# Softmax maximum carried as rows of the query stack in two of three attentions, one broadcast copy on VectorE, output bias on GpSimd, later weights in six portions

## What is computed

```
x = x + _L0_xattn_ref(_layernorm(x, axis=-1), ctx_1024, ctx_1024, ...)   # 16 heads of 8
x = x + _L0_ffn_ref(...)                                                 # 8 experts, top 2
x = x + _L1_xattn_ref(_layernorm(x, axis=-1), ctx_1024, ...)             # the same, with rotary positions
x = x + _L1_ffn_ref(...)                                                 # quantised
x = x + _L2_xattn_ref(_layernorm(x, axis=-1), ctx_1024, ctx_1024, ...)   # one key/value head for 16 query heads, biases
x = x + _L2_ffn_ref(...)
x = x + _L3_xattn_ref(...)                                               # one head of 128
x = x + _L3_ffn_ref(...)
# a 16-head attention:
scores = einsum('bhqd,bhkd->bhqk', q, k) / sqrt(8)
out = einsum('bhqk,bhkd->bhqd', softmax(scores), v) @ Wo.T (+ bo in layer 2)
```

## Time and profile before

| what | value |
|---|---|
| median of three runs | 1574.77 us (1566.39 to 1575.15) |
| the profiled execution | 1575.81 us, its span 1574.0 us |
| PE, DVE, ACT, POOL busy over the span | 81%, 60%, 44%, 32% |
| row maxima on DVE (L501) | x384, 687 ns each |
| second matmuls with `pick_head` on PE (L629) | x1536, 512 of them in each of A0, A1, A2 |
| A0: first score matmul to last `scoresT` | 44.0 to 244.8 us |
| A1: the same | 600.1 to 826.5 us |
| A2: the same | 913.6 to 1112.3 us |

### The profile page before, as it was taken

The page is one execution under the profiler, slowest core; times in us unless marked ns, Lnnn a source line. Parts: engine busy times, 40 slices in busy tenths (PEclk is TensorE's granted clock), DMA queues, the critical chain, the costliest instruction groups (busy, mean ns, idle before and its releaser), DMA issues. The chain is left out here.

```text
span 1574.0 us, 38722 instructions
## 1 busy us (share of the span) xinstructions
PE 1268.9 (81%) x12718; PEld 1023.4 (65%) x12718; DVE 947.0 (60%) x2946; ACT 688.8 (44%) x1442; POOL 496.8 (32%) x564
## 2 busy tenths in 40 slices
PE   3899995439979958889996689999799865489991
PEld 1677883328869926677783367778577665478981
DVE  2567765624544347778855567777477767676452
ACT  1456662125535503345563346666333353144440
POOL 2222201541445255422301132220111112776065
PEclk9999996559999967789998879999799987599996
DMA  5775633011223236436420044332200031134342
GB/s 141 172 217 149 172 99 121 27 54 49 80 75 103 80 104 155 108 94 164 109 79 1 14 113 126 81 101 70 81 0 0 22 113 67 61 111 123 106 140 77
DMA packets 120187, 147.93 MB, mean 94 GB/s; under 512 B 14560, under 2 KB 100726, under 8 KB 113956
## 3 DMA queue, kind: packets, MB, share of 16 engines
q1 hardware_dynamic: 111876, 129.97, 29.4%
q0 software_dynamic: 8192, 16.46, 3.8%
HBM read 95.79 MB, written 50.92 MB: 93 GB/s over the span
## 5 line engine op out<-in xcount | busy, mean ns | idle before, releaser
L501 DVE TENSOR_REDUCE A_neg_max<-A_s_bank 128x4 f32<-128x512 f32 x384 | 260.1, 687 | 139.3 <-PE A_s_bank L614 135.2
L376 ACT ACTIVATE A_probsT<-A_st_bank 128x512 f32<-128x512 f32 x384 | 227.6, 598 | 84.8 <-PE A_st_bank L629 78.1
L627 PE MATMUL A_st_bank<-A_q_stack,A_k_stack 72*128 72x128 bf16 x1536 | 226.1, 225 | 2.0 <-ACT A_max_partsT L370 1.1
L629 PE MATMUL A_st_bank<-A_max_partsT,pick_head 96*128 96x128 bf16 x1536 | 225.6, 224 | 0.0
L614 PE MATMUL A_s_bank<-A_k_stack,A_q_stack 72*128 72x128 bf16 x1536 | 158.2, 229 | 22.3 <-DVE A_neg_max L501 18.0
L627 PEld LDWEIGHTS A_st_bank<-A_q_stack,A_k_stack 72*128 72x128 bf16 x1536 | 157.2, 104 | 28.1 <-issue 26.3
L629 PEld LDWEIGHTS A_st_bank<-A_max_partsT,pick_head 96*128 96x128 bf16 x1536 | 154.4, 101 | 9.6 <-issue 8.0
L614 PEld LDWEIGHTS A_s_bank<-A_k_stack,A_q_stack 72*128 72x128 bf16 x1536 | 112.1, 102 | 34.1 <-DVE A_neg_max L501 23.8
L640 PE MATMUL A_pv_bank<-A_probsT,A_v_pad 128*32 128x128 f32 x3072 | 128.9, 285 | 0.0
L1933 ACT ACTIVATE E_h<-E_h_bank,w_L_b 128x256 f32<-128x256 f32 x184 | 76.9, 472 | 85.7 <-PE E_h_bank L2036 84.8
L2036 PE MATMUL E_h_bank<-E_xT,E_w_u 128*128 128x256 f32 x368 | 92.1, 396 | 7.9 <-issue 7.2
(11 more groups left out here) (363 smaller groups left out, 2775.8 us busy)
## 6 DMA issues: line engine op xcount, KB each, us to landing
A_q_stack<-q_scratch SPq DMA_DIRECT2D x48, 576.0 KB
A_k_stack<-k_scratch SPq DMA_DIRECT2D x32, 576.0 KB
q_scratch<-A_q_parts SPq DMA_DIRECT2D x48, 192.0 KB, 2.3
A_ctxT<-in_ctxT SPq DMA_DIRECT2D x33, 256.0 KB, 6.8
E_xe<-slots_in SPq DMA_DIRECT2D x53, 128.0 KB, 2.1
slots_out<-E_ye SPq DMA_DIRECT2D x53, 128.0 KB, 1.7
k_scratch<-A_k_parts SPq DMA_DIRECT2D x32, 192.0 KB
q_scratch<-A_q_parts SPq DMA_DIRECT2D x48, 128.0 KB, 2.2
```

What stands on the lines that cost most here:

```text
L376: act.activation(probsT[n % 2][:, c * HQ:(c + 1) * HQ, :], st_bank[c % 2][:, :].rearrange("k (a q) -> k a q", a=HQ), ACT.Exp, scale=scale) ...
L501: dve.tensor_reduce(neg_max[:, c * HQ:(c + 1) * HQ], s_bank[c % 2][:, :].rearrange("q (a k) -> q a k", a=HQ), AX.X, ALU.max, negate=True). ...
L627: pe.matmul(dst, k_stack[slot][:, h % kheads, at:at + S], q_stack[slot][:, h, at:at + S], start=True, stop=False)
L629: last = pe.matmul(dst, core.pick_head[:, h, :], max_partsT[n % 2][:, :], start=False, stop=True)
```

## The change

In A0 and A2 (`spread = not rope`) the second matmul goes away. The stacks have 128 rows: 72 of data, 24 plus 32 more in the query stack and 56 in the key stack. Rows 96 to 127 of the query stack hold the maxima (high parts of the 16 heads, then low parts), the same rows for every head; rows 72 to 127 of the key stack hold a constant of zeros and ones (`pick_rows`) that picks a head's two rows. The constants are made once at the start, stored to DRAM (`pick_dram`) and loaded by SP into the four slots (`constants`). Per batch one DVE copy (`spread_max`) repeats the 32 rows of `max_rows` for 16 heads; it stands behind `divide` and `place(0)`. `scores` still uses 72 rows. For the constants to fit, A2's key stack gets a copy of the key rows for every head, in three DMAs per half. A2's output bias is added to x by POOL, four batches at a time, not by DVE batch by batch. `load_rest` is cut into six portions, one ahead of each of the groups 2 to 7, largest weights first. A1 keeps its second matmul.

```diff
-        k_stack = [sb(f"k_stack{i}", [COMBO, kheads, HALF], BF16) for i in range(4)]
+        k_stack = [sb(f"k_stack{i}", [S if spread else COMBO, NH, HALF], BF16) for i in range(4)]
...
+                    if shared:
+                        rows = dram[p][half].rearrange("i d t -> (i d) t")
+                        span = rows.shape[1]
+                        each = bass.AP(tensor=rows.tensor, offset=rows.offset, ap=[[span, 3 * DH], [0, NH], [1, span]])
+                        for i in range(3):
+                            sp.dma_start(dest[i:COMBO:3, :, :], each).then_inc(stack_loaded[slot], 16)
...
+            def constants(slot):
+
+                if spread:
+                    flat = lambda t: t.rearrange("r h t -> r (h t)")
+                    sp.dma_start(flat(k_stack[slot][COMBO:S, :, :]), core.pick_dram).then_inc(stack_loaded[slot], 16)
+                    sp.dma_start(flat(q_stack[slot][COMBO:hi, :, :]), core.pick_dram[0:hi - COMBO, :])\
+                        .then_inc(stack_loaded[slot], 16)
...
             load_ctx(0, 0, 0)
             prep(0)
+            constants(2)
+            constants(3)
             prep(1)
-            if load_rest:
-                load_rest(sp)
             for g in range(2, NG):
+                if load_rest:
+                    load_rest(sp, g - 2, NG - 2)
                 prep(g)
...
+            def add_bias(g):
+
+                if shared_kv:
+                    pool.wait_ge(xn_done, g + 1)
+                    core.settle(pool)
+                    x4 = core.x_group(g).rearrange("t (b d) -> t b d", b=GB)
+                    pool.tensor_tensor(x4, x4, shared_kv[3][:, None, :].to_broadcast([S, GB, D]), ALU.add)\
+                        .then_inc(bias_added, 1)
...
+            def spread_max(b, n):
+
+                dve.wait_ge(mt_copied, b + 1)
+                dve.tensor_copy(q_stack[n // 2 % 4][MAX_ROWS, 0:BY_DVE, n % 2 * S:(n % 2 + 1) * S],
+                                max_rows[n % 2][MAX_ROWS, None, :].to_broadcast([2 * NH, BY_DVE, S])).then_inc(m_spread, 1)
...
                     divide(b)
-                    add_bias(b)
                     place(0)
+                    if spread and has_scores(b + 1):
+                        spread_max(b + 1, n + 1)
...
                 if c == 0:
-                    pe.wait_ge(mt_copied, b + 1)
+                    pe.wait_ge(m_spread if spread else mt_copied, b + 1)
...
-                    pe.matmul(dst, k_stack[slot][:, h % kheads, at:at + S], q_stack[slot][:, h, at:at + S],
-                              start=True, stop=False)
-                    last = pe.matmul(dst, core.pick_head[:, h, :], max_partsT[n % 2][:, :], start=False, stop=True)
+                    last = pe.matmul(dst, k_stack[slot][:, h, at:at + S], q_stack[slot][:, h, at:at + S],
+                                     start=True, stop=spread)
+                    if not spread:
+                        last = pe.matmul(dst, core.pick_head[:, h, :], max_rows[n % 2][:, :], start=False, stop=True)
...
+                sp.wait_ge(picked, 1)
+                sp.dma_start(core.pick_dram, wide_pick[:, :, :].rearrange("r h t -> r (h t)")).then_inc(pick_stored, 16)
                 sp.wait_ge(x_loaded, 16)
+                sp.wait_ge(pick_stored, 16)
...
+                dve.tensor_copy(wide_pick[:, :, :], narrow_pick[:, :, None].to_broadcast([S - COMBO, NH, HALF]))\
+                    .then_inc(picked, 1)
```

More of the change, by code:

```diff
@@ L90, in multi_head_attention @@
     kd = DH if shared_kv else D
-    kheads = 1 if shared_kv else NH
+    vheads = 1 if shared_kv else NH
+    spread = not rope
+    MAX_ROWS = slice(S - 2 * NH, S) if spread else slice(0, 96)
+    BY_DVE = NH
     if rope:
@@ L144, in multi_head_attention @@
         neg_max = sb("neg_max", [S, NH], F32)
-        max_parts = sb("max_parts", [S, 96], BF16)
-        max_partsT = [sb(f"max_partsT{i}", [96, S], BF16) for i in range(2)]
+        max_parts = sb("max_parts", [S, MAX_ROWS.stop], BF16)
+        max_rows = [sb(f"max_rows{i}", [MAX_ROWS.stop, S], BF16) for i in range(2)]
+        hi, lo = MAX_ROWS.start, MAX_ROWS.start + (NH if spread else 32)
         outT = sb("outT", [128, HQ, S], F32)
@@ L347, in _ @@
                     split_rest(pool, own, q_f, q_parts, D, g + 2, QL, q_lead, q_split)
+            for g in range(2):
+                add_bias(g)
             first = own.n
@@ L369, in copy_max @@
                 act.wait_ge(mt_ready, b + 1)
-                act.copy(max_partsT[q][:, :], wo_bank16[0:96, 0:S]).then_inc(mt_copied, 1)
+                if spread and not (isinstance(b, int) and b < 2):
+                    act.wait_ge(m_spread, b - 1)
+                act.copy(max_rows[q][MAX_ROWS, :], wo_bank16[MAX_ROWS, 0:S]).then_inc(mt_copied, 1)
             def exps(b, n, c):
@@ L522, in divide, with add_x @@
                                   sums[:, :, :, None].to_broadcast([S, 4, HQ, DH]), ALU.mult).then_inc(o_norm, 1)
-            def add_bias(b):
-                if shared_kv:
-                    own.did(dve.tensor_tensor(core.x_tile(b - 1), core.x_tile(b - 1), shared_kv[3], ALU.add))
-            def add_x(b):
-                if shared_kv:
-                    own.wait()
+            def add_x(b, n=0):
+                if shared_kv and n % GB == 1:
+                    dve.wait_ge(bias_added, add_x.it * 2 + n // GB + 1)
                 dve.wait_ge(wo_ready, START + b + 1)
@@ L640, in probs_v @@
                     last = pe.matmul(pv_bank[a * VW:(a + 1) * VW, c * S:(c + 1) * S],
[L641 removed]
+                                     v_pad[p][:, n % GB, h % vheads, :], probsT[n % 2][:, h, :], start=True, stop=True)
                 if c == 3:
@@ L2747, in program, with load_rest @@
         first_loads = [load for load in loads if load[2] in needed_first]
-        rest_loads = [load for load in loads if load[2] not in needed_first]
-        def load_rest(sp):
-            for dst, src, _ in rest_loads:
+        size = lambda load: math.prod(n for _, n in load[0].ap)
+        rest_loads = sorted((load for load in loads if load[2] not in needed_first), key=size, reverse=True)
+        def load_rest(sp, part=0, parts=1):
+            for dst, src, _ in rest_loads[part::parts]:
                 sp.dma_start(dst, src).then_inc(rest_loaded, 16)
@@ L2760, in load_expert @@
             sp.dma_start(exp_w1[:, at], ap["L0_exp_w1"].rearrange("d e f -> d (e f)")[:, at]).then_inc(exp_w1_loaded, 16)
-        with nc.sbuf_tensor("wide_pick", [96, NH, S], F32) as wide_pick, nc.Block() as block:
-            first_loads.append((wide_pick[:, :, :], ap["pick_head"], "wide_pick"))
+        picked = ctx.enter_context(nc.semaphore("picked"))
+        pick_stored = ctx.enter_context(nc.semaphore("pick_stored"))
+        with nc.sbuf_tensor("narrow_pick", [S - COMBO, NH], F32) as narrow_pick,\
+                nc.sbuf_tensor("wide_pick_head", [96, NH, S], F32) as wide_pick_head,\
+                nc.sbuf_tensor("wide_pick", [S - COMBO, NH, HALF], BF16) as wide_pick, nc.Block() as block:
+            first_loads.append((narrow_pick[:, :], ap["pick_rows"], "narrow_pick"))
+            first_loads.append((wide_pick_head[:, :, :], ap["pick_head"], "wide_pick_head"))
             @block.sync
@@ L2842, in shape_constants @@
     c = {"ident": np.eye(128, dtype=np.float32)}
+    pick = np.zeros((56, 16), np.float32)
+    for part in range(2):
+        pick[24 + 16 * part:40 + 16 * part, :] = np.eye(16, dtype=np.float32)
+    c["pick_rows"] = pick
     pick = np.zeros((96, 16, 128), np.float32)
```

58 lines of the change are left out of this document (35 added, 23 removed).

## The result

The changed kernel takes 1563.65 us (median of 14 runs, 1559.65 to 1567.09) where the kernel before, on the same chip, takes 1574.47 (14 runs): a ratio of 0.9936, 95% interval 0.9925 to 0.9947. It is faster, by 10 to 11 us and not by the 41 of the forecast. That is inside the wide range of 1514 to 1566 us, at its slow end, which was there for a rival, and outside the forecast's own 1523 to 1548. The profiled execution took 1563.3 us, with a span of 1561.4.

What follows compares the result with a forecast made beforehand. PE's instruction stream was taken to bound A0 and A2. Gains of 20 and 5.5 us in A0 and 25 in A2, less 9.5 of costs, made 41: from 1575.8 to 1535 us, own range 1523 to 1548, wide range 1514 to 1566.

Steps and rivals of the forecast that it cites:

- PE's work: A0 and A2 loops: sixteen fewer matmuls save PE 0.94 us per batch, 3.76 per group, leaving 20.8 in A0.
- The copy's length: The new DVE copy of 2048 columns, each batch in A0 and A2: taken as 0.70 us.
- The rivals with 1.22 and 2.2 us: Slower DVE copy: at 1.22 us the kernel takes 1566 us, chance 0.14; at 2.2 us 1631, chance 0.07.
- The copy itself waits for ACT's copy of the maxima: DVE copy in the loop: ACT's copy ends at 105.38, the division at 105.36, so waiting costs nothing.
- Waits of 1.2 us per group: A0 loop: PE and DVE do not hide each other fully; 1.2 us of waits make the group 22.0 us.
- The loss mostly passes on: A2: the 0.19 us per batch lost behind POOL moves to `normalise` in the second batch, which meets the same instruction.
- DVE per plain batch: Batch without preparation: DVE carries 3.5 us, with the copy and its semaphore 4.3, against PE's 4.43.
- Bias: A2: moving the output bias from DVE to POOL gains DVE 0.2 to 0.3 us per batch; group 22.1 us.
- Portions: A0: later weights in portions let the context load go out near 64 us, recovering the whole 5.5 us lost.
- Starts: Start costs: opening 3 us, first `scoresT` 1.5 in each of two attentions, A2's key loads 3.5; 9.5 in all.
- the stacks have slack too: Weights in portions, A0: the stack loads can bear the new order of DMAs, so the 5.5 us is taken whole.
- the second one: POOL or DMA takes part back: 0.3 us per copy behind POOL, 19 us, 1554; or late A2 stacks, 1553; chance 0.16.

Runs made afterwards that it cites:

- half_copy: The changed kernel with the DVE copy writing 8 of 16 heads, constants for the rest: 0.9922 of the kernel before, 12.0 us less.
- pool_waits: The changed kernel with POOL's key split waiting until the group's normalised x is written: 0.9924 of the kernel before, 15.4 us less.

## Why the prediction was wrong, and where it was right

- **PE's work** (right, in part by luck): 20.8 us a group forecast, 21.1 measured (95.07 of 108 us, times 23.93). The matmuls of 128 rows cost nothing extra: they come 0.056 us from start to start, those before 0.058. But the 20.8 were the old period less 3.76 and held 0.7 us of PE's waits (it was busy 105.04 of 108 us, 23.9 per group), so by busy time 20.1 were due. The other 1.0 us fits the way of counting, since before each wait the last matmul counts to its end, 0.22 us, and not to the next start; that is an estimate.
- **The copy's length** (right): 0.70 us forecast, 0.69 measured where nothing is in its way, 0.42 for 1024 columns. The rivals with 1.22 and 2.2 us fall.
- **"The copy itself waits for ACT's copy of the maxima, which ends at 105.38 where the division ends at 105.36, so this costs nothing"** (wrong, the step that failed first, and the largest cause that was shown). It is true of the batch whose rows were read. In the third batch ACT's two query copies stand ahead of that copy, and it costs 1.62 us, with 0.37 more because the copy then meets POOL; taking it out gave 0.89 us of period in A0 and 10 us in all. Before the change nothing on DVE hung on this ACT copy, so the trace of before could show no wait; the order of ACT, with place(0) ahead of `copy_max`, could.
- **Waits of 1.2 us per group** (wrong): 2.9 in A0, 3.1 in A2. Of the 1.93 us over the forecast of A0, the ACT order is 0.89, POOL in the way of `normalise` 0.64, and 0.40 stay in the run with both repaired; of the 2.51 of A2 they are 0.56, 0.60 and 1.34. Over 8 groups of each, the loops missed the forecast by 35.5 us: 21.6 of them are these two causes, and the cause of the other 14 stays open. The time is only some 30 us off because the portions gave 4 us more than forecast.
- **"The loss mostly passes on"** (right in kind, not carried into the sum): POOL's key split lengthens `normalise` from 1.11 to 1.75 us. It was named, and the sum has no term of its own for it in A0.
- **DVE per plain batch** (a little low): 4.3 forecast, 4.55 measured back to back, above PE's 4.43. The two engines were taken as 19.5 and 20.8 us; by the measured rows DVE's is 18.2 + 1.5 + 1.1 = 20.8 without any delay, so the slack of 1.3 us was not there. This alone doesn't explain the miss: half_copy took 1.1 us of work off DVE and gave 0.28 in A0, all in the batch without preparation. In the others it is the waits of one engine for another that count.
- **Bias** (a little high): 0.2 to 0.3 us per batch taken, 0.67 per group (0.17 per batch) measured with the copy.
- **Portions** (right, 5.5 us in the kernel before): 5.5. In the changed kernel without them the context load comes later still, so that they keep off 9 to 10. From 84 to 90 us, where the granted clock was 0.54, it is 1.00 in the changed kernel, as forecast.
- **Starts** (the sum right, its terms less so): 9.5 forecast, 9.4 measured. The opening was taken at 3 us and cost 1.9 (SP's first A0 load at 18.53, not 16.62), of which 1.5 are left at the first scores; the first `scoresT` of A2 cost 2.9 where 1.5 was taken. Group 1's stacks went out 8 us later, which was not foreseen ("the stacks have slack too").
- **Rivals**: the 19 us of the second one come nearest in kind (POOL takes a part back), yet the larger part of what was shown was ACT's order, which no rival named. DMA did not take part in the steady loop: PE had no stack wait from 92 to 200 us at a DMA share of 0.68, nor from 950 to 1080 at 0.61. Ahead of it PE did wait for stacks, 1.58 us at 69.7 in A0, 2.6 and 1.6 at 905 and 931 in A2, which the prediction had named as a sign of being wrong.

The sum by measured terms: 8 x 0.60 + 8 x 0.66 + 5.5 - 9.4 = 6.2, against 10 to 11. With the portions at the 9.9 us that they are worth here by the ratios (0.9999 - 0.9936, of 1574.47) it is 10.6.

## What to carry to other kernels

When an engine takes over a step, its new instruction inherits a producer: follow that producer's order through every phase of the loop (here four batches), not the one batch with the cleanest rows. Where two engines come within some per cent of each other, add up both with start-to-start times over a whole period before calling one the bound, since a delay may then reach the time; and take a little work off each in turn to see in which batches it does. And cost the starts as carefully as the loop: here they ate what 512 x 2 removed matmuls gave.

## What the runs showed of the hardware that was not expected

- A VectorE copy whose source repeats (32 x 128 read 16 times, bfloat16 to bfloat16) runs as fast as a plain one would: 0.69 us for 2048 columns and 0.42 for 1024, 0.26 ns per column, half of the 0.514 of the cast from float32. The Trainium skill ("VectorE: DVE Perf Modes", the perf-mode tier table) gives 693 ns for such a copy without repetition, and the trace agrees.
- The same copy took up to 1.08 us, and `normalise` (four instructions) 1.75 and not 1.11, where a POOL instruction of 1.16 us ran. The Trainium skill ("SBUF — State Buffer", on the shared port pair) has them exclude each other for a whole instruction; the trace agrees: the first of the four instructions of `normalise` began at 138.14 us, 0.26 us into POOL's, and ended at 139.12, 0.08 us behind POOL's end, 0.99 us long where it takes 0.34 in pool_waits. The copy at 146.07 met POOL's instruction when 0.51 us of it were left and lost 0.37.
- Issuing one store took SP 5.69 us with two slots' constants issued ahead of it and 0.70 without, so what stands ahead can show up as the length of an issue, and SP issues nothing else meanwhile. It doesn't explain every long issue: the second such store took 4.04 us with them, 3.69 without, and 3.12 in the kernel before.
